# Last layer of a four-layer graph network: edges ranked by groups of four nodes, outer products summed per group in place of a weight matrix per edge

## The reference, cut to what matters

```python
N_NODES, D, EH, STEPS = 6250, 32, 128, 6
h = out = relu(n_feat @ lin0_w.T + lin0_b)
eh = relu(e_feat @ en1_w.T + en1_b)                  # 200000 x 128
w_e = (eh @ en2_w.T + en2_b).reshape(-1, D, D)       # a 32x32 matrix for each edge
for _ in range(STEPS):
    msg = einsum('ei,eio->eo', out[src], w_e)
    agg = segment_sum(msg, dst, num_segments=n_nodes) + conv_bias
    m = relu(agg)
    h = gru_cell(m, h, gru_wih, gru_whh, gru_bih, gru_bhh)
    out = h
```

## Time and profile before

| what | value |
|---|---|
| median of 3 runs | 34,158.61 us |
| lowest to highest | 34,123.43 to 34,195.55 us |
| span of the profiled execution, first to last instruction | 34,991.4 us |
| mean granted TensorE clock in it | 0.912 |
| last layer in it, 18,070 to 34,985 us | 16,915 us |
| gating layer, 12,492 to 17,976 us | 5,484 us |
| attention layer, 10,657 to 12,269 us | 1,612 us |

### The profile page before, as it was taken

One profiled execution on the slowest core, in us unless ns is written; L12 is line 12 of the kernel. 1 busy time (PEld: TensorE's weight loads), 2 busy tenths in 40 slices (PEclk: granted clock), 3 DMA queues, 4 the chain that ended last, 5 costly groups with the idle time before them and its releaser, 6 DMA issues. The chain is left out here.

```text
span 34991.4 us, 506188 instructions
## 1 busy us (share of the span) xinstructions
PE 24995.2 (71%) x109314; PEld 18873.1 (54%) x109315; DVE 23964.8 (68%) x32356; ACT 18324.4 (52%) x67317; POOL 18961.6 (54%) x21358
## 2 busy tenths in 40 slices
PE   0000006776668877777779999998999999999998
PEld 0000003442226743333348878887887887887887
DVE  6500006777887645545558988888888888888888
ACT  0000003443335622222248877887887877887887
POOL 1777764665660045555545555555555555555555
PEclk9999996558998778888889999999999999999999
DMA  2111126772111045565568888888888888888887
GB/s 87 27 26 29 26 71 213 225 224 63 24 24 19 19 140 196 196 187 195 193 203 321 324 295 313 317 315 299 317 322 299 322 311 296 318 317 295 315 318 287
DMA packets 2649695, 7252.58 MB, mean 207 GB/s; under 512 B 1572986, under 2 KB 2063642, under 8 KB 2227516
## 3 DMA queue, kind: packets, MB, share of 16 engines
q1 hardware_dynamic: 1845260, 6330.76, 48.4%
q0 software_dynamic: 694720, 730.46, 9.5%
q10 hardware_dynamic: 109680, 190.99, 1.5%
HBM read 6103.15 MB, written 1147.36 MB: 207 GB/s over the span
## 5 line engine op out<-in xcount | busy, mean ns | idle before, releaser
L1726 POOL DMA_INDIRECT e_got<-round_table,e_index x9696 | 9180.6, 947 | 7198.1 <-ACT e_weight L1776 4316.6
L1897 DVE TENSOR_TENSOR e_weight<-e_weight,e_wide 128x2048 f32<-128x2048 f32 x7272 | 9716.1, 1392 | 178.1 <-ACT e_wide L1772 81.1
L1827 PE MATMUL e_node<-e_weight,e_hot 128*128 128x256 f32 x38784 | 9301.5, 391 | 733.4 <-DVE e_weight L1897 395.2
L1776 ACT ACTIVATE e_weight<-e_weight,e_got 128x32 f32<-128x32 f32 x38784 | 8469.1, 306 | 212.4 <-issue 108.6
L1827 PEld LDWEIGHTS e_node<-e_weight,e_hot 128*128 128x128 f32 x38784 | 7300.7, 194 | 1870.0 <-issue 856.8
L1827 PE MATMUL e_wide<-e_weight,e_hot 128*128 128x256 f32 x19392 | 4707.6, 386 | 408.6 <-DVE e_msg L1900 248.6
L1553 PE MATMUL g_weight_ps<-w,g_hidden 128*128 128x512 f32 x6464 | 3476.8, 681 | 1353.2 <-DVE g_weight L1594 1059.3
L752 POOL DMA_INDIRECT g_got<-second_table,g_index x3232 | 3061.2, 947 | 2269.6 <-DVE g_load L1601 1322.7
L1827 PEld LDWEIGHTS e_wide<-e_weight,e_hot 128*128 128x128 f32 x19392 | 3723.0, 193 | 1039.2 <-issue 346.7
L1594 DVE TENSOR_TENSOR g_weight<-g_weight_ps,en_b 128x1024 f32<-128x1024 f32 x1616 | 1956.9, 1223 | 2359.9 <-remote 1221.7
L777 ACT ACTIVATE e_hot<-iota,neglo 128x128 f32<-128x128 f32 x9696 | 3075.8, 388 | 911.8 <-DMA harmonics<-harm 883.4
(11 more groups left out here) (306 smaller groups left out, 32098.7 us busy)
## 6 DMA issues: line engine op xcount, KB each, us to landing
e_weight<-edge_weights SPq DMA_DIRECT2D x2424, 2048.0 KB
edge_weights<-g_weight SPq DMA_DIRECT2D x808, 1024.0 KB
e_got<-round_table,e_index POOLq DMA_INDIRECT x9696
edge_hidden<-h_hidden ACTq DMA_DIRECT2D x404, 256.0 KB
g_hidden<-edge_hidden SPq DMA_DIRECT2D x808, 128.0 KB
g_got<-second_table,g_index POOLq DMA_INDIRECT x3232
s_rows<-edge_attr SPq DMA_DIRECT2D x284, 176.0 KB
edges_by_src<-pad ACTq DMA_DIRECT2D x16, 2020.0 KB, 35.0
```

Source lines behind the costliest of these rows:

```text
L1726: g_.indirect_dma_start(got[q][:, u, :], None, k.round_table, bass.IndirectOffsetOnAxis(ap=index[q // 2][:, at:at + 1], axis=0)).then_inc( ...
L1776: half = a_.activation(w, w, ACT.Copy, scale=got[q][:, V - 1, f:f + 1])
L1827: last = t_.matmul(into, hot[q][:, u, :], weight[q][:, u, m * FOLD:(m + 1) * FOLD], start=m == 0, stop=m == 3)
L1897: v.tensor_tensor(w, w, x, ALU.mult).then_inc(done, 1)
```

## The change: what it does, and the diff

A new stage, `refine_edges`, runs after the sorts. It ranks the edges of each block again, by groups of four destination nodes (32 groups in a block and one kind for padding): for each of the 33 kinds DVE marks the edges of the kind, PE counts them and, in a second pass, forms sums over the mark, and DVE runs a scan along the tiles. Then small tables are made: a pair of a tile and a four-node group is an item; a group gets one item for each tile that it touches, so 1616 + 1568 items, padded to 3200.

`harmonic_layer` makes the edge units with edges on the partitions, by four matmuls of 128 columns in place of one of 512, the bias by an added row of ones. `attention_layer` carries these units to their new places: SP loads a chunk of them, POOL copies in two indices and scatters four tiles of 528-byte rows into `edges_by_node`, in all 1616 scatters. `gating_layer` loses its products with en2, its bias addition and its stores.

`edge_conditioned_layer` is written anew. A batch is four items. DVE makes, per item, a 128x128 tile: the gathered row in the place of each of four nodes where the edge goes to that node, else zero. PE multiplies it with the 129 edge units (4 matmuls a batch), ACT copies the result, PE turns it (4 transposes), ACT copies it again, and every eight batches PE applies en2 in 33 accumulating matmuls of 32 columns, and one more matmul spreads the 128 message rows over nodes, which DVE adds to totals. There are 800 batches a round. The ring of edge rows holds 16 tiles, and a chunk of it is 270 KB; the source indices for the gathers are a column of these rows.

```diff
@@ gating_layer @@
-                for u in range(HALF):
-                    pe.wait_ge(biased, n * HALF + (s * chunks * HALF + u + 1))
-                    for m in range(2):
-                        last = nc.tensor.matmul(weight_ps[u][:, m * 512:(m + 1) * 512], hidden[q][:, u * P:(u + 1) * P],
-                                                k.w2[:, s * u, m * 512:(m + 1) * 512], start=True, stop=True)
...
-                    v.tensor_tensor(weight[q][:, u, :], weight_ps[u][:, :], k.en2_b[:, s * u, :], ALU.add).then_inc(biased, 1)
...
@@ refine_edges, second pass @@
+            for n in range(KINDS):
+                pe.wait_ge(masked, KINDS + n + 1)
+                pe.wait_ge(spread_out, n + 1)
+                if n:
+                    pe.wait_ge(taken, n)
+                for c, e in spans:
+                    mm(ps[:, 2048 + c:2048 + e], k.ones[:, :], mask[n % 2][:, c:e], start=True, stop=True)
+                    mm(ps[:, c:e], before[:, :], mask[n % 2][:, c:e], start=True, stop=False)
+                    last = mm(ps[:, c:e], wide_start[n % 2][0:NB, :], of_block[0:NB, c:e], start=False, stop=True)
+                last.then_inc(placed, 1)
...
+                dve.wait_ge(placed, n + 1)
+                step(v.tensor_tensor_scan(along[:, :], keep[:, :], ps[:, 2048:2048 + NT], 0.0, ALU.mult, ALU.add))
+                step(v.tensor_tensor(along[:, :], along[:, :], ps[:, 0:NT], ALU.add))
+                dve.sem_inc(taken, 1)
+                step(v.tensor_tensor(along[:, :], along[:, :], mask[n % 2][:, :], ALU.mult))
+                step(v.tensor_tensor(place[:, :], place[:, :], along[:, :], ALU.add))
...
@@ attention_layer, POOL @@
+                    if not opening:
+                        pool.wait_ge(scattered[q], i * (16 * U))
+                    g_.tensor_copy(inner[q][:, :, E_SRC:E_DST + 1], k.ends[:, bass.ds(c * U, U), :]).then_inc(inner_full, 1)
+                    g_.tensor_copy(to[q][:, :], k.finer[:, bass.ds(c * U, U)]).then_inc(inner_full, 1)
+                    pool.wait_ge(inner_full, c * 2 + 2)
+                    pool.wait_ge(inner_in[q], i * 16 + 16)
+                    pool.sem_inc(scattering, 1)
+                    for u in range(U):
+                        g_.indirect_dma_start(k.fine_rows, bass.IndirectOffsetOnAxis(ap=to[q][:, u:u + 1], axis=0),
+                                              inner[q][:, u, :], None).then_inc(scattered[q], 16)
...
@@ edge_conditioned_layer, SP @@
+            def arrive(r, i, q):
+
+                n = (r * k.TURNS + i) * 16 + 16
+                sp.wait_ge(loaded[q], n)
+                sp.sem_inc(looked, 1)
+                sp.wait_ge(landed[q], n * U)
+                sp.sem_inc(ready, 1)
...
+                for q in range(Q):
+                    sp.wait_ge(done, least[q] + r * B)
+                    sp.dma_start(ring[:, q * U:(q + 1) * U, :], rows[:, bass.ds((i * Q + q) * U, U), :]).then_inc(loaded[q], 16)
+                    sp.sem_inc(freed, 1)
+                    if q >= 1 or not opening:
+                        arrive(r, *((i, q - 1) if q >= 1 else (i - 1, Q - 1)))
...
@@ edge_conditioned_layer, POOL @@
+                pool.wait_ge(freed, r * chunks + i * Q + (q + 1))
+                pool.wait_ge(loaded[q], (r * k.TURNS + i) * 16 + 16)
+                pool.sem_inc(passed, 1)
+                g_.tensor_copy(index[q][:, :], ring[:, q * U:(q + 1) * U, E_SRC]).then_inc(copied, 1)
...
+                for q in range(Q):
+                    fetch(r, i, q, range(U // 2))
+                    if not (last and q == Q - 1):
+                        fill(r, *((i, q + 1) if q < Q - 1 else (i + 1, 0)))
+                    fetch(r, i, q, range(U // 2, U))
...
@@ edge_conditioned_layer, PE and DVE @@
+                for x in range(U):
+                    to = n % 2 * 1024 + x * 256
+                    last = t_.matmul(outer_ps[:, to:to + FULL], spread[n % 4][:, x, :],
+                                     ring[:, bass.ds(at[x], 1), 0:FULL].rearrange("p a f -> p (a f)"), start=True, stop=True)
...
+                    last = t_.transpose(turn_ps[:, to:to + P], outer[h][:, n % EACH * U + x, 0:P], k.ident[:, :])
...
+                for i in range(D):
+                    t_.matmul(msg_ps, turned[h][:, i, :], k.w2[:, i * D:(i + 1) * D], start=i == 0, stop=False)
...
+                    last = v.scalar_tensor_tensor(
+                        spread[n % 4][:, x, :].rearrange("p (j i) -> p j i", j=NEAR),
+                        nodes[:, bass.ds(item * NEAR, NEAR)].unsqueeze(2).to_broadcast(wide),
+                        ring[:, bass.ds(at[x], 1), E_DST:E_DST + 1].rearrange("p a f -> p (a f)"),
+                        got[:, bass.ds(at[x], 1), :].to_broadcast(wide), ALU.is_equal, ALU.mult)
```

841 lines of the change are left out of this document (549 added, 292 removed).

## The result

| what | before | after |
|---|---|---|
| median of four runs | 34,177 us | 41,796 us |
| ratio, 95% interval | | 1.222 (1.220 to 1.225) |
| span of the profiled execution | 34,991.4 us | 41,746.7 us |
| mean granted TensorE clock | 0.912 | 0.716 |

The changed kernel is slower by 22%, where 5% was forecast and 38.5 ms was the upper end. One of the four runs after took 42,753 us at a mean clock of 0.643; it counts in the median and not in the ratio. First the profile's page: busy time of each engine with its share and instructions, then the line on the chain of work that ended last, by engine, then the row of the ring loads among the DMA issues (KB each, median us to landing).

A forecast was written before the change was run, and what follows sets the result against it. Compute on the streamed weight matrices was taken to bound the kernel before. 34.99 + 1.1 + 0 + 0.93 - 1.2 + 0.12 + 0.9 = 36.84 ms, scaled by 0.976 to 35.95 ms, slower by 5%; range 33.4 to 38.5.

The forecast's parts named there:

- The last layer: Edge-conditioned layer, six rounds: 17.8 ms in place of 16.9, +0.9 ms, bound by the SP-POOL loop, then PE in last blocks.
- the gating layer: Gating layer: -1.2 ms, POOL's four gathers and half an index copy setting 5.2 us a chunk; range -1.0 to -1.28.
- The ranking stage: New stage after the sorts: +1.1 ms, hidden by nothing, range 0.85 to 1.4.
- The harmonic layer: Harmonic layer: 0, PE moving the same columns with extra weight loads overlapped; range -0.1 to +0.2 ms.
- The tables: Seven DMAs at the last layer's start, some in small elements: +0.12 ms, 0.25 at most.
- The attention layer: Attention layer: +0.93 ms, POOL's two copies and four scatters taking 6.3 us a chunk; range +0.85 to +1.05.
- way of putting them together: Last layer: per block the larger of 7.1 us loop and 2.8 us batch prices, plus 50 us a round, giving 17.8 ms.
- loop's turn: Last layer, SP and POOL: ring load, copy and restart, gather, landing sum to 7.1 us a chunk; ends 5.65 and 8.2.
- PE's price of a batch: Last layer: outer products 1.17, transposes 0.66, en2 products 1.0, together 2.8 us; PE takes over in the last 18 blocks.
- Rival 2: PE's clock falls where it idles: at 0.78, last layer 19.4 ms, kernel 37.5, chance 0.15; 1.2 GHz throughout, 42.8, chance 0.04.
- The scaling: Whole sum times 0.976, the profiled execution being longer than the median of the runs: 36.84 becomes 35.95 ms.
- Rival 1: Last layer's loop turn only 5.65 us: layer 15.5 ms, kernel 33.7 ms scaled, faster by 1.3%; chance 0.2.

The follow-up runs named there:

- the run with two products of 33: Changed kernel with 31 of the 33 matmuls that apply en2 to eight batches left out on PE: 40,166 us, ratio 1.176.
- the last run with SP signalling: Changed kernel with eight ring slots, operands of the 33 products exchanged, products given six at a time between batches, SP waiting for landed gathers: 39,730 us, ratio 1.143.
- products exchanged and spread: Changed kernel with eight ring slots, POOL signalling chunks ready, operands of the 33 products exchanged and products given six at a time between batches: 39,014 us, ratio 1.141.
- the runs with POOL's signal: Five variants of the changed kernel where POOL, not SP, waits for landed gathers; with that edit alone 42,400 us, ratio 1.241.

## Why the prediction was wrong, point by point

The sum in the profile's terms was 36.84 ms, and the profiled execution took 41.75. The last layer is 4.5 ms of the difference, the gating layer 0.53; the other stages come to -0.1 together.

**The ranking stage: right.** 1.10 ms forecast, 1.099 measured. That the two agree to 1 us is luck, since the parts cancel: the first pass took 0.18 ms where 0.1 was taken, the second 0.79 where 0.85 was. **The harmonic layer: right**, 2,633 us against 2,567, +0.07 within the range. **The tables** took 0.08 ms where 0.12 was taken. **The attention layer: right in mechanism**, 6.05 us a chunk with POOL as the bound where 6.3 was taken, +0.83 ms and so just below the range of 0.85 to 1.05. The restart behind the copies is 0.84 us, as taken; but the first copy follows the fourth scatter at once, which saves the 0.3 us that stands between two scatters.

**The gating layer: -0.66 in place of -1.2.** The step that failed is "That is 5.0 + 0.2 = 5.2 us a chunk", which has POOL's gathers alone set the time and the other engines hidden beside them. POOL's gathers do take 1.25 us each, as the earlier trace rows said, and 0.95 of it is the instruction; but the layer is at 5.98 us a chunk and not 5.2, since DVE is held up for some 16 us once in four chunks at 0.70 us an instruction, or PE where DVE has less to do. POOL's wait for DVE's gate, 707 us, is 0.9 us a chunk; without it an estimate from these two rows gives 5.1. No row read of before shows this: there the same additions on DVE (L1611) had 14.5 us of idle time put down to issue, now (L1826) 2,036. The Trainium skill, "Runtime: NRT & Kernel Launch", section "Instruction fetch mechanics", says that a jump to a target outside the pages held makes the engine fetch a page of 16 KiB by DMA before it goes on. The trace speaks against that here: of the changed kernel's DMA rows from 14,500 to 19,250 us, two queues carry instructions, and they moved one packet each in 4.75 ms, some 200 turns:

```profile
q8 instruction: 1, 0.02, 0.0%
q14 instruction: 1, 0.01, 0.0%
```

**The last layer: +5.4 in place of +0.9.** Two terms were mis-sized, and the way of putting them together was wrong. An estimate tells how much each is worth: with the turn at 8.05 us and the batch at 3.37, both as measured, the prediction's rule of the larger price per block gives some 20.4 ms, and 17.8 with its own two terms (tiles per block by the formula of the inputs). So the sizes make some 2.6 of the 4.5 ms and the rule 1.9. With eight slots the layer took 20.3 ms: there the rule comes out.

The *loop's turn* was 7.1 us by its four rows and is 7.95 to 8.2. Step by step: ring load 2.45 forecast, 2.6 to landing and 2.73 to POOL's copy; copy and restart 0.93, measured 0.75; third to fourth gather 1.25, measured 1.27; last gather to SP's next issue 2.47, measured 2.87. That is 7.62. The rest is SP's loading of four limits into registers with the instructions behind it, 1.9 us once in four chunks, 0.5 a chunk; it was in the range as 0.3 "for SP's register load and hand-overs". The upper end of the turn, 8.2, was thus about right as a forecast. The Trainium skill's fit for a DMA, "DMA: Bandwidth & Descriptors", section "Anatomy of one DMA — SWDGE (gpsimd) path", which the prediction set aside because a row of 1.9 us lay below it, gave an estimate of 2.62 for the ring load; the trace, 2.6, agrees with it, although the section is on DMAs issued by POOL and this one is issued by SP. In the run with two products of 33 the layer is 20.7 ms, with 0.6 of slot waits left, and in the last run with SP signalling, which has none, 19.9 in place of 17.8: the loop alone makes some 2.1 of the 4.5 ms.

*PE's price of a batch* was 2.8 us (2.6 to 3.2) and is 3.37: 16,192 us over 4,800 batches. By form, from the page's groups, four outer products 1.56 us where 1.17 was taken, transposes 0.79 for 0.66, products 1.22 for 1.0 (they overlap, so the three come to more than 3.37); the rows that it took are from the high clock, and the layer's is 0.71. Rival 2 had this mechanism, with a chance of 0.15 at a clock of 0.78, and put 3.5 us a batch and 37.5 ms on it; its size of a batch was nearly right.

The *way of putting them together* is the third step that failed, worth nearly as much as the loop's turn: "Taking for each block the larger of" the loop's and PE's price. That holds only where a ring lies between the two that never empties or fills. With four slots the two wait for one another in turn: SP waited 2.1 ms for slots, most of it in blocks where the rule has none, and eight slots brought the layer down by 2.0 ms with the same loop and the same work on PE. The exchanged operands, by their clock, brought 1.05 with four slots.

What the prediction ruled out was right as far as it went: DVE's and ACT's rows, 2.6 and 2.3 us a chunk, do not bound the layer. With POOL signalling the compute side took 9.4 us a chunk beside 6.9 of PE's busy time; PE, ACT and DVE wait for one another there, and instructions come late that come in time in the changed kernel. What the changed kernel's compute side takes by itself was not measured; with its products exchanged and spread it is 7.9 us at most.

**The scaling was unfounded.** The sum was multiplied by 0.976, since the profiled execution of before was 2.4% above the median of its runs. After the change the two stand 0.1% apart. The factor took 0.9 ms off the sum. The kernel before took 34,194, 34,198 and 34,727 us as the median of later comparisons, so 1.6% between two chips occurs without any difference in the kernel. Whether the 2.4% came from profiling or from the chip is not shown.

**The rivals.** Rival 1 (a turn of 5.65 us) was wrong at each step: the copy's restart is 0.56 us and not 0.16, the load 2.73 and not 1.9, the last landing 2.87 and not 2.1. Its prices were low ends, from rows of other sizes. The forecast's own limit, "I am wrong if ... the granted clock of the last layer is under 0.85 (rival 2)", was met: 0.71. But rival 2 at its 0.78 would have been 37.5 ms and not 41.8.

The pieces add up: 4.53 (last layer) + 0.53 (gating) + 0.07 - 0.10 - 0.04 (harmonic, attention, tables) + 0.89 (scaling) = 5.88 ms, and 41.80 less 35.95 is 5.85.

**What is left open.** Why instructions come at 0.70 us in stretches, and on which engine, was not found: neither the number of jumps nor DVE's number of instructions decides it, and in the gating layer no packets of the instruction queues go with it. Whether the recording of the trace has a part in it was not tested. It cost the gating layer 0.6 to 0.7 ms. In the changed kernel's last layer it is nearly absent on DVE and PE; SP has 508 such records of 26,612 there, 0.36 ms if all of them lay in the loop's chain. In the runs with POOL's signal its part was not separated from the waits between engines.

## What to carry to other kernels

Where a change puts a loop of loads and gathers through two queues in place of a stream that ran ahead, price the loop by its own DMA sizes and by everything that its issuing engine does in a turn, register loads too; the two sides of a ring of few slots do not hide one another fully, so forecast more than the larger of the two (here 22.3 ms in place of 20.4 with four slots, and 20.3 with eight), or ask for more slots first. And before a variant's time is taken as the price of one side, look whether its engines carry out their instructions as they do in the kernel to be explained: here moving one wait from SP to POOL made DVE's and PE's instructions late, and the variant gained nothing although it opened the loop.

## What the runs showed of the hardware

PE's clock fell while PE was busy. The rows are stretches of the changed kernel round the row of 33 products (128 columns of weights, 32 columns streamed): length, PE busy (instructions), and so on, with the clock before the last two numbers.

```profile
22501.50:22504.00 2.50, 2.50 (x26) 2.50 (x23) 2.31 (x8) 1.10 (x3) 0.19 (x1) 1.00 0.37 108
22504.00:22507.00 3.00, 3.00 (x20) 3.00 (x19) 0.00 (x0) 0.00 (x0) 1.91 (x2) 0.64 0.03 5
22507.00:22510.00 3.00, 3.00 (x16) 3.00 (x16) 1.45 (x5) 0.00 (x0) 1.89 (x2) 0.50 0.23 38
```

PE is busy in all three, and the granted clock goes from 1.00, 2.4 GHz, to 0.50, 1.2 GHz, in the middle of the row; the records of the products start 0.112 us apart before and 0.213 after. With the operands exchanged, 32 columns of weights and 128 streamed, the layer's clock was 0.82 in place of 0.71 although PE was busy for less of it, 66% in place of 72%. So the clock does not follow PE's busy share alone. The prediction had it fall where PE idles. The Trainium skill, "TensorE: Matmul & The Clock Gate", section "Part 1: The HAM clock gate", says that activity releases the throttle; a busy row that loses the clock is not what one reads out of it.

And an engine with nothing to wait for is not always at work: in the changed kernel's gating layer there were stretches of some 16 us a turn in which DVE's instructions came 0.70 us apart or twice that, where the same ones took 0.01 to 0.1 elsewhere in the loop (a register load 0.34). In the last layer DVE had 8 to 79 such records in the five runs in which SP signals and 771 to 3,100 in the five in which POOL does.
